# Writing out the loops of two transformer stacks and splitting 17 of every 35 wide products in two

## The chip, the cores and the metric

The kernel runs on one core of a Trainium2 chip. The metric is the device time in microseconds (us) from the kernel's start to its end. TensorE is called PE here (its weight loads PEld), VectorE DVE, ScalarE ACT, GpSimd POOL, and SP is the engine that issues the transfers.

## The reference, cut to what matters

Four layers are applied one after the other to x of shape (4, 512, 128): a retention block, a stack, a mixer with a recurrence, and the same stack again with the same weights. The change touches the stacks alone. A stack has six layers:

```python
for i in range(DEPTH):                                   # DEPTH = 6
    x = attn_layer(shift_tokens(x), Wqkv[i], ...) + x    # 16 heads of 64, window 32
    x = ffn_layer(shift_tokens(x), ...) + x              # 128 -> 341 (twice) -> 128, gated
```

The attention layer projects x to queries, keys and values (128 to 3 x 1024), normalises and rotates queries and keys, takes the softmax over a band of 64 keys, weighs the values and projects back. The feed-forward layer normalises, multiplies into two halves of 341 (a gate and a linear part), and multiplies back. Everything is float32.

## The kernel before

A stack is worked tile by tile. A tile is 128 rows of x; a sequence of 512 rows is four tiles, a layer 16, a stack 96. The kernel calls four tiles a group (`Group`, 24 in a stack). `slots` runs 96 + 16 slots, and in slot N each engine works on parts of the tiles N-3 to N-10: a software pipeline with a fixed order in each engine, written out by hand in `slot`, with one body for each place T = 0..3 of a tile in its group. PE's part of it, tile by tile:

- `project` (line 608): six products of 128 rows by 512 columns, for the parts k0, q0, k1, q1, v0, v1; `PARTS` numbers them 0 to 5.
- `turn` (line 617): four transposes for each of k0, q0, k1, q1.
- `scores` (line 632): 64 small products, 64 or 32 wide, which in float32 are 128 matrix instructions. `weigh` (line 655) is another 64, again 128 instructions.
- `project_out` (line 668): eight accumulated products of 128 columns.

Once in four tiles come `center` (line 675), `variance` (line 682), `up` (line 691, six products) and `down` (line 701, three products), each with 512 columns. So four tiles hold 24 + 1 + 1 + 6 + 3 = 35 products of 512 columns. A float32 product is two matrix instructions (the transposes are one), and each matrix instruction comes with a weight load of its own.

Behind PE, `rotate` on DVE (lines 1080 and 1082) reads each projection of a query or key from PSUM; `square` on ACT (line 881) reads the same bank when DVE has; a bank is given back to PE after that. The four work banks are handed out by the table `BANK`.

`slots` writes slots 0 to 15 out, then runs a hardware loop of two turns with a body of 32 slots, and then writes the last 32 slots out. So the loop holds 64 of the 112 slots of a stack:

```python
            run_slots(0, 0, 0, 0, 16)
            with eng.Fori(0, 2) as pair:
                run_slots(32 * pair + 16, 8 * pair + 4, 2 * pair + 1, 1, 32)
            run_slots(16 * (DEPTH - 1), 4 * (DEPTH - 1), DEPTH - 1, 1, 16 + 16)
```

In the loop the value that a wait compares with comes from a register, and `apart` puts a semaphore increment between two such waits; in code that is written out it does nothing. SP has a loop of its own over layers 1 to 4. `run` is 0 in the first stack and 1 in the second.

Of the kernel before, what the change touches and what calls it, by code (L numbers as in the profile page):

```python
# [14 lines left out]
P = 128  # L15
DIM = 128
BATCH, SEQ = 4, 512
# [3 lines left out]
DEPTH, HEADS, HD, WINDOW = 6, 16, 64, 32  # L21
# [3 lines left out]
TILES = DEPTH * BATCH * SEQ // P  # L25
# [314 lines left out]
RSQRT_SHIFT = 16  # L340
TABLE = "natural_log_exp_and_others"
GELU_TABLE = "gelu_and_others"

Group = namedtuple("Group", ("number", "layer", "row", "pair", "half"))
# [2 lines left out]
def ffn_stack(nc, shared, w):  # L348

    xo, ident, rot, mask = shared["x"], shared["ident"], shared["rot"], shared["mask"]  # L350
    with ExitStack() as ctx:
# [124 lines left out]
        def slots(eng, body):  # L476

            def run_slots(tile, group, layer, odd, slots_run):  # L480
                for n in range(slots_run):
                    def of(lag, k=n // 4):
                        return Group(group + (k - lag), layer + (k - lag) // 4, (k - lag) % 4, (k - lag) % 2,
                                     (odd + (k - lag) // 4) % 2)

                    def at(lag, n=n):
                        return tile + (n - lag), (n - lag) % 4, of(0, (n - lag) // 4)
                    body(tile + n, n % 4, group + n // 4, at, of)

            run_slots(0, 0, 0, 0, 16)  # L490
            with eng.Fori(0, 2) as pair:
                run_slots(32 * pair + 16, 8 * pair + 4, 2 * pair + 1, 1, 32)
            run_slots(16 * (DEPTH - 1), 4 * (DEPTH - 1), DEPTH - 1, 1, 16 + 16)

        block = ctx.enter_context(nc.Block())

# [1 line left out]
        def _(sp):  # L498
# [80 lines left out]
            load_mlp(0)  # L579
            sp.wait_ge(consts_set, N_CONSTS * (run + 1))  # L580
            layer_loads(0, True, False)
            with sp.Fori(1, DEPTH - 1) as layer:
                layer_loads(layer, False, False)
            layer_loads(DEPTH - 1, False, True)
            sp.wait_ge(wo_in, 16 * (layer0 + DEPTH))
# [11 lines left out]

        @block.tensor
        def _(pe):
            def project(t, T, g, c):  # L600
                if not live(t):
                    return
                if c == FIRST_IN and T == 0:
                    wait_x(pe, g.number - BATCH)
                    apart(pe, t)
                    pe.wait_ge(qkv_in, (g.layer + (layer0 + 1)) * 256)
                col = 512 * PARTS[c]
                pe.matmul(work[(BANK["p_" + c][T] + g.row) % 4][:, :], xst[:, g.row, P * T:P * (T + 1)],  # L608
                          w_qkv[:, g.half, col:col + 512], start=True, stop=True).then_inc(done["proj_" + c], 1)

            def turn(t, T, g, c):
                if not live(t):
# [58 lines left out]
            def center(g):  # L671
                if not live_group(g):
                    return
                wait(pe, "mid_set", 4 * g.number + 3)
                pe.matmul(work[(BANK["ct"] + g.row) % 4][:, :], center_m[:, :], mshift[:, g.pair, 0:SEQ], start=True, stop=True  # L675
                          ).then_inc(done["pe_center"], 1)

            def variance(g):
                if not live_group(g):
                    return  # L680
                wait_group(pe, "center_sq", g)
                pe.matmul(work[(BANK["va"] + g.row) % 4][:, :], mean_m[:, :], c_sq[:, :], start=True, stop=True  # L682
                          ).then_inc(done["pe_var"], 1)

            def up(g, kind, k):
                if not live_group(g):
                    return
                wait_group(pe, "xg_set", g)
                n = min(P, HID - P * k)
                bank = work[(BANK[("wa" if kind == "lin" else "wg") + str(k)] + g.row) % 4]  # L690
                pe.matmul(bank[0:n, :], w_1[:, g.half, 3 * (kind == "lin") + k, 0:n], x_c[:, :], start=True, stop=True  # L691
                          ).then_inc(done[f"pe_{kind}{k}"], 1)

            def down(g):
                if not live_group(g):
# [1913 lines left out]
```

## Time and profile before

| | |
|---|---|
| median of 3 runs | 3644.86 us (3643.79 to 3651.21) |
| the profiled execution: its time | 3648.2 us |
| its span, first to last instruction | 3646.4 us |
| granted TensorE clock, mean | 0.967 |
| first stack, about | 98 to 1665 us |
| second stack, about | 2083 to 3646 us |

"Span" is the time from the first to the last instruction of the profiled execution; its own time is 1.8 us longer. Where a position is given below (as at 1324.17) it is in us from the start of that span. Busy time of PE is modelled from the starts of pipelined instructions.

### The profile page before, as it was taken

To read this page: it belongs to the slowest core of one execution; us is meant where nothing else is said; L and a number is where in the kernel's file an instruction comes from. 1 tells how busy PE (TensorE), PEld (TensorE's weight loads), DVE (VectorE), ACT (ScalarE), POOL (GpSimd) and SP (SyncE) were. 2 spreads that over 40 slices of the span, in tenths; PEclk is the share of its full clock that TensorE was granted. 3 is DMA by queue.
4 is the path that set the end of the run, shared out by engine and by line. 5 is a ranking of instruction groups with operands and counts; after the bars stand their busy time and mean duration, and the time that the engine had idled before them with its cause. 6 is when DMAs were issued, how large, how long until landed. Compare 5 with 4: busy or idle time off the path is not lost. (4 is left out here: it accounts for less than half of the span.)

```text
span 3646.4 us, 153624 instructions
## 1 busy us (share of the span) xinstructions
PE 3373.7 (93%) x60144; PEld 2186.3 (60%) x60144; DVE 3341.6 (92%) x11899; ACT 2049.2 (56%) x3659; POOL 2706.3 (74%) x2440
## 2 busy tenths in 40 slices
PE   6799999999999999987699689999999999999997
PEld 4366666666666666652466446666666666666664
DVE  6899999999999999965799799999999999999995
ACT  2456666656665666644422155666666566666663
POOL 1788888888888888843144288888888888888882
PEclk9899999999999999998799699999999999999999
DMA  1233333333333333320000123333333333333332
GB/s 44 61 89 83 74 89 75 90 78 79 91 76 76 87 80 71 72 66 16 1 1 0 36 49 88 79 89 79 74 93 75 77 84 82 73 89 77 72 72 65
DMA packets 151851, 250.83 MB, mean 69 GB/s; under 512 B 42688, under 2 KB 73408, under 8 KB 150976
## 3 DMA queue, kind: packets, MB, share of 16 engines
q1 hardware_dynamic: 151104, 240.75, 27.7%
q8 instruction: 484, 7.93, 1.0%
q14 instruction: 263, 2.15, 0.2%
HBM read 38.21 MB, written 1.05 MB: 11 GB/s over the span
## 5 line engine op out<-in xcount | busy, mean ns | idle before, releaser
L608 PE MATMUL stack_work<-stack_w_qkv,stack_xst 128*128 128x512 f32 x2304 | 1173.6, 615 | 26.9 <-ACT stack_sq L881 16.7
L1337 POOL TENSOR_TENSOR stack_roped<-stack_rot_c,stack_rot_s 128x512 f32<-128x512 f32 x768 | 980.6, 1289 | 260.1 <-DVE stack_rot_s L1082 135.0
L1347 POOL TENSOR_TENSOR stack_roped<-stack_roped,stack_rnorm 128x512 f32<-128x512 f32 x768 | 791.5, 1044 | 162.4 <-DVE stack_rnorm L1114 162.4
L881 ACT ACTIVATE stack_sq<-stack_work 128x512 f32<-128x512 f32 x768 | 457.3, 595 | 735.0 <-DVE stack_rot_s L1082 727.5
L1080 DVE TENSOR_TENSOR stack_rot_c<-stack_work,rot_tables 128x512 f32<-128x512 f32 x768 | 517.0, 673 | 56.5 <-PE stack_work L608 52.0
L608 PEld LDWEIGHTS stack_work<-stack_w_qkv,stack_xst 128*128 128x128 f32 x2304 | 387.3, 193 | 300.5 <-issue 226.5
L1082 DVE TENSOR_TENSOR stack_rot_s<-stack_work,rot_tables 128x512 f32<-128x512 f32 x768 | 519.3, 676 | 1.1 <-issue 1.1
L1091 DVE TENSOR_REDUCE stack_ssq<-stack_sq 128x8 f32<-128x512 f32 x768 | 512.4, 672 | 3.3
L1125 DVE CUSTOM_DVE_ANT_0 stack_s_m<-stack_bank_s,band 128x64 f32<-128x64 f32 x3072 | 469.5, 215 | 30.1 <-PE stack_bank_s L632 26.4
L617 PEld LDWEIGHTS stack_work<-ident,stack_roped 128*128 128x128 f32 x3072 | 354.1, 141 | 167.4 <-issue 143.5
L617 PE MATMUL stack_work<-ident,stack_roped 128*128 128x128 f32 x3072 | 436.4, 277 | 19.3 <-ACT stack_sq L881 11.6
L1363 POOL TENSOR_TENSOR stack_s_m<-stack_s_m,stack_inv 128x512 f32<-128x512 f32 x384 | 412.6, 1074 | 37.8 <-DVE stack_inv L1143 37.8
L1355 POOL TENSOR_TENSOR stack_s_m<-stack_s_m,stack_smax 128x512 f32<-128x512 f32 x384 | 401.6, 1046 | 37.3 <-DVE stack_smax L1125 35.2
L655 PEld LDWEIGHTS stack_bank_o<-stack_p_pairs,stack_v_even 64*64 64x64 f32 x12288 | 330.0, 134 | 155.8 <-issue 155.6
L668 PEld LDWEIGHTS stack_work<-stack_o_t,stack_w_o 128*128 128x128 f32 x3072 | 364.5, 192 | 77.4 <-issue 63.8
L632 PEld LDWEIGHTS stack_bank_s<-stack_k_t,stack_q_t 64*32 64x32 f32 x24576 | 276.6, 105 | 206.2 <-issue 200.1
L655 PE MATMUL stack_bank_o<-stack_p_pairs,stack_v_nat 64*64 64x32 f32 x12288 | 378.2, 219 | 16.6 <-issue 16.5
L655 PE MATMUL stack_bank_o<-stack_p_pairs,stack_v_even 64*64 64x32 f32 x12288 | 378.8, 220 | 12.4 <-issue 8.8
L668 PE MATMUL stack_work<-stack_o_t,stack_w_o 128*128 128x128 f32 x3072 | 368.2, 275 | 5.2 <-issue 4.7
L632 PE MATMUL stack_bank_s<-stack_k_t,stack_q_t 64*32 64x64 f32 x24576 | 318.5, 225 | 48.0 <-issue 47.6
L655 PEld LDWEIGHTS stack_bank_o<-stack_p_pairs,stack_v_nat 64*64 64x64 f32 x12288 | 333.4, 135 | 20.2 <-issue 20.1
L907 ACT COPY stack_q_t<-stack_work 128x512 f32<-128x512 f32 x384 | 226.8, 591 | 169.0 <-PE stack_work L617 168.2
(255 smaller groups left out, 5093.2 us busy)
## 6 DMA issues: line engine op xcount, KB each, us to landing
stack_v_even<-stack_v_nat SPq DMA_DIRECT2D x768, 128.0 KB, 2.4
stack_p_pairs<-stack_p_turned SPq DMA_DIRECT2D x1536, 64.0 KB
stack_w_qkv<-table_ffn_qkv SPq DMA_DIRECT2D x192, 96.0 KB
stack_w_o<-table_ffn_wo SPq DMA_DIRECT2D x12, 512.0 KB, 3.9
stack_w<-table_ffn_w SPq DMA_DIRECT2D x12, 384.0 KB, 3.2
stack_w<-table_ffn_w SPq DMA_DIRECT2D x12, 192.0 KB, 3.0
x_outer<-L_attn_a_X SPq DMA_DIRECT2D x4, 256.0 KB, 8.1
ret_xpos<-table_xpos SPq DMA_DIRECT2D x1, 1024.0 KB, 7.5
```

Of the source, the lines that this page charges most:

```text
L608: pe.matmul(work[(BANK["p_" + c][T] + g.row) % 4][:, :], xst[:, g.row, P * T:P * (T + 1)], w_qkv[:, g.half, col:col + 512], start=True, st ...
L617: last = pe.transpose(bank[:, P * n:P * (n + 1)], roped[:, CHUNKS.index(c), T % 2, P * n:P * (n + 1)], ident[:, :])
L632: last = pe.matmul(bank_s[j][WINDOW * n:WINDOW * (n + 1), 64 * hp:64 * hp + 64], q_t[rows, T % 2, hp, WINDOW * n:WINDOW * (n + 1)], k_t[ro ...
L655: last = pe.matmul(bank_o[HD * odd:HD * (odd + 1), two, at:at + WINDOW], values[:, 2 * m + j, :], p_pairs[rows, T % 2, odd_window, j, 2 * ...
L668: last = pe.matmul(bank[:, 0:P], w_o[:, g.half, n, :], o_t[:, T % 2, n, :], start=n == 0, stop=n == PAIRS - 1)
L881: act.activation(sq[:, i % 2, :], work[(BANK["p_" + c][T] + g.row) % 4][:, :], ACT.Square).then_inc(done["squared_" + c], 1)
L1080: dve.tensor_tensor(rot_c[:, i % 2, :].rearrange("p (h d) -> p h d", h=8), src.rearrange("p (h d) -> p h d", h=8), cosine, ALU.mult)
L1082: dve.tensor_tensor(rot_s[:, i % 2, :].rearrange("p (h f d) -> p h f d", h=8, f=2), src.rearrange("p (h f d) -> p h f d", h=8, f=2)[:, :, ...
L1091: dve.tensor_reduce(ssq[:, T % 2, i, :], sq[:, i % 2, :].rearrange("p (h d) -> p h d", h=8), AX.X, ALU.add).then_inc(done["summed_" + c], 1)
L1125: last = dve.tensor_tensor_reduce(s_m[:, T % 2, j, hp, :], bank_s[j][:, 64 * hp:64 * hp + 64], mask[:, first:first + 2 * WINDOW], 1.0, LOW ...
L1337: pool.tensor_tensor(roped[:, i, T % 2, :], rot_c[:, i % 2, :], rot_s[:, i % 2, :], ALU.add).then_inc(done["roped_" + c], 1)
L1347: pool.tensor_tensor(r, r, rnorm[:, T % 2, i, :].unsqueeze(2).broadcast_to([P, 8, HD]), ALU.mult).then_inc(done["united_" + c], 1)
```

## The change

The two hardware loops become straight code: all 112 slots of a stack in every engine, and all six layers on SP. In each group 17 of the 35 products with 512 columns are issued as two products of 256 columns into the two halves of the same PSUM bank (`HALVED`; `center` and `variance` are not in it). In the first stack the first 25 projections in the order of tiles (tiles 0 to 3 and k0 of tile 4) and in the second stack the first 17 are issued as four products of 128 columns (`QUARTERED`). The semaphore is raised by the last piece, so what DVE and ACT do is as it was. And v0 and v1 get a wait for the layer's weights at the first tile of a group, which only k0 had.

```diff
+HALVED = {
+    ("gate", 1), ("gate", 2), ("k0", 1), ("k0", 2), ("k0", 3), ("k1", 0),
+    ("k1", 1), ("lin", 0), ("lin", 1), ("q0", 1), ("q0", 3), ("q1", 0),
+    ("q1", 2), ("v0", 1), ("v1", 1), ("v1", 2), ("v1", 3),
+}
+QUARTERED = (25, 17)
...
-            run_slots(0, 0, 0, 0, 16)
-            with eng.Fori(0, 2) as pair:
-                run_slots(32 * pair + 16, 8 * pair + 4, 2 * pair + 1, 1, 32)
-            run_slots(16 * (DEPTH - 1), 4 * (DEPTH - 1), DEPTH - 1, 1, 16 + 16)
+            run_slots(0, 0, 0, 0, TILES + 16)
...
-            with sp.Fori(1, DEPTH - 1) as layer:
+            for layer in range(1, DEPTH - 1):
                 layer_loads(layer, False, False)
...
+            def spans(pieces):
+                return [slice(SEQ // pieces * k, SEQ // pieces * (k + 1)) for k in range(pieces)]
...
-                col = 512 * PARTS[c]
-                pe.matmul(work[(BANK["p_" + c][T] + g.row) % 4][:, :], xst[:, g.row, P * T:P * (T + 1)],
-                          w_qkv[:, g.half, col:col + 512], start=True, stop=True).then_inc(done["proj_" + c], 1)
+                elif c[0] == "v" and T == 0:
+                    pe.wait_ge(qkv_in, (g.layer + (layer0 + 1)) * 256)
+                bank = work[(BANK["p_" + c][T] + g.row) % 4]
+                pieces = 4 if 6 * t + PARTS[c] < QUARTERED[run] else 2 if (c, T) in HALVED else 1
+                for s in spans(pieces):
+                    col = 512 * PARTS[c] + s.start
+                    last = pe.matmul(bank[:, s], xst[:, g.row, P * T:P * (T + 1)],
+                                     w_qkv[:, g.half, col:col + 512 // pieces], start=True, stop=True)
+                last.then_inc(done["proj_" + c], 1)
...
-                pe.matmul(bank[0:n, :], w_1[:, g.half, 3 * (kind == "lin") + k, 0:n], x_c[:, :], start=True, stop=True
-                          ).then_inc(done[f"pe_{kind}{k}"], 1)
+                for s in spans(2 if (kind, k) in HALVED else 1):
+                    last = pe.matmul(bank[0:n, s], w_1[:, g.half, 3 * (kind == "lin") + k, 0:n], x_c[:, s], start=True, stop=True)
+                last.then_inc(done[f"pe_{kind}{k}"], 1)
```

## Rows read from the trace of the kernel before

**Rows 1.** The page: each engine's busy us, share and instructions.

```profile
PE 3373.7 (93%) x60144; PEld 2186.3 (60%) x60144; DVE 3341.6 (92%) x11899; ACT 2049.2 (56%) x3659; POOL 2706.3 (74%) x2440
```

**Rows 2.** The page's transfer queues: kind, packets, MB, share of 16 engines.

```profile
q8 instruction: 484, 7.93, 1.0%
```

**Rows 3.** Windows, 21 groups of each stack: us, busy (count) by engine, clock, DMA.

```profile
239.89:1545.11 1305.22, 1272.38 (x25657) 838.68 (x25656) 1263.14 (x4829) 819.69 (x1470) 1108.60 (x1009) 1.00 0.34 80
2220.92:3531.07 1310.15, 1272.37 (x25657) 839.25 (x25656) 1260.78 (x4829) 819.69 (x1470) 1107.60 (x1008) 0.99 0.34 80
```

**Rows 4.** Windows of single groups, line 675's start to the next.

```profile
487.18:547.94 60.76, 60.67 (x1223) 39.72 (x1222) 60.41 (x232) 38.88 (x70) 52.80 (x49) 1.00 0.36 82
673.28:733.27 59.99, 59.99 (x1224) 39.69 (x1223) 58.59 (x230) 38.75 (x70) 51.38 (x48) 1.00 0.38 93
...
1423.26:1483.92 60.66, 60.56 (x1223) 39.78 (x1222) 60.31 (x231) 38.87 (x70) 52.96 (x49) 1.00 0.31 71
...
300.96:364.47 63.51, 60.38 (x1224) 40.07 (x1223) 61.08 (x231) 39.31 (x70) 54.41 (x50) 1.00 0.35 84
...
733.27:799.90 66.63, 62.52 (x1224) 40.59 (x1223) 60.96 (x231) 39.09 (x70) 52.77 (x49) 0.97 0.33 75
2719.70:2786.08 66.38, 62.36 (x1224) 40.43 (x1222) 59.52 (x230) 39.08 (x70) 51.20 (x48) 0.97 0.33 75
```

**Rows 5.** Waits of PE in 239.9 to 1545.1: us in total, times, longest.

```profile
PE stack_bank_s L632 <- issue: 19.0, 19, 1.7
PE stack_bank_o L655 <- issue: 8.4, 11, 1.4
```

**Rows 6.** Timeline of PE at two of its gaps: start, us, line, shape [idle before].

```profile
1324.17 0.34 PE L632 MATMUL stack_bank_s<-stack_k_t,stack_q_t 64*32 64x64 f32 x16 [0.97 <-issue]
1386.27 0.31 PE L632 MATMUL stack_bank_s<-stack_k_t,stack_q_t 64*32 64x64 f32 x7 [1.54 <-issue]
```

**Rows 7.** Windows from gap to gap.

```profile
1324.16:1386.26 62.10, 60.55 (x1257) 40.20 (x1257) 61.44 (x232) 39.00 (x70) 53.48 (x50) 1.00 0.34 80
1386.26:1495.77 109.51, 108.22 (x2135) 70.65 (x2135) 106.48 (x405) 67.49 (x121) 91.83 (x85) 0.98 0.33 75
```

**Rows 8.** Transfer queues in the window 1321.5 to 1324.3.

```profile
q8 instruction: 1, 0.02, 2.2%
```

**Rows 9.** Timeline of PE: the end of `scores` in two groups.

```profile
667.70 1.55 PE L632 MATMUL stack_bank_s<-stack_k_t,stack_q_t 64*32 64x64 f32 x120
670.38 0.32 PE L632 MATMUL stack_bank_s<-stack_k_t,stack_q_t 64*32 64x64 f32 x8 [1.14 <-issue]
...
1418.94 1.74 PE L632 MATMUL stack_bank_s<-stack_k_t,stack_q_t 64*32 64x64 f32 x128
```

**Rows 10.** Timeline at the loop's turn back in the first stack.

```profile
768.66 1.96 PE L608 MATMUL stack_work<-stack_w_qkv,stack_xst 128*128 128x512 f32 x2 [2.97 <-DMA stack_w_qkv<-table_ffn_qkv]
```

**Rows 11.** Timeline of PE: products of 512, 128 and 256 columns, one burst.

```profile
1003.98 1.02 PE L608 MATMUL stack_work<-stack_w_qkv,stack_xst 128*128 128x512 f32 x2
...
1005.71 1.88 PE L608 MATMUL stack_work<-stack_w_qkv,stack_xst 128*128 128x512 f32 x4
...
1012.83 1.51 PE L632 MATMUL stack_bank_s<-stack_k_t,stack_q_t 64*32 64x64 f32 x128
...
1031.19 3.94 PE L668 MATMUL stack_work<-stack_o_t,stack_w_o 128*128 128x128 f32 x32
1882.54 7.54 PE L2147 MATMUL scan_bank<-scan_seen,ident 128*128 128x256 f32 x16
1889.89 3.63 PE L2136 MATMUL scan_bank<-mix_kept_kkb,mix_spread 128*128 128x256 f32 x16
1893.37 1.03 PE L2136 MATMUL scan_bank<-mix_kept_r,mix_spread 128*128 128x256 f32 x4
```

**Rows 12.** Waits in 1423 to 1483, a group without a gap in PE.

```profile
ACT stack_sq L881 <- DVE stack_rot_s L1082: 14.9, 13, 2.4
...
PEld stack_work L668 <- ACT stack_sq L881: 0.9, 1, 0.9
```

More of the change, by code:

```diff
@@ L674, in center @@
                 wait(pe, "mid_set", 4 * g.number + 3)
-                pe.matmul(work[(BANK["ct"] + g.row) % 4][:, :], center_m[:, :], mshift[:, g.pair, 0:SEQ], start=True, stop=True
-                          ).then_inc(done["pe_center"], 1)
+                bank = work[(BANK["ct"] + g.row) % 4]
+                for s in spans(2 if ("center", 0) in HALVED else 1):
+                    last = pe.matmul(bank[:, s], center_m[:, :], mshift[:, g.pair, s], start=True, stop=True)
+                last.then_inc(done["pe_center"], 1)
             def variance(g):
@@ L681, in variance @@
                 wait_group(pe, "center_sq", g)
-                pe.matmul(work[(BANK["va"] + g.row) % 4][:, :], mean_m[:, :], c_sq[:, :], start=True, stop=True
-                          ).then_inc(done["pe_var"], 1)
+                bank = work[(BANK["va"] + g.row) % 4]
+                for s in spans(2 if ("variance", 0) in HALVED else 1):
+                    last = pe.matmul(bank[:, s], mean_m[:, :], c_sq[:, s], start=True, stop=True)
+                last.then_inc(done["pe_var"], 1)
             def up(g, kind, k):
```

## The prediction

> **What bounds the kernel now.** I read the page first. PE is busy 93% and DVE 92% of the span [rows 1]; an average says no more than that both are near their limit somewhere, so I cut the trace into periods. Line 675 (`center`) runs once in four tiles, and from one of its starts to the next is one group of a stack. Each stack has 21 such periods in its steady part, 1305.2 and 1310.2 us long [rows 3]: 62.15 and 62.39 us a group, 62.27 in the mean. The 42 periods make 2615.4 us, 72% of the span. The rest is the filling and draining of the two pipelines, the retention and the mixer, where PE waits for other engines most of the time.
>
> The single periods show what the mean hides [rows 4]. PE's work is the same in each, 1222 matrix instructions. The shortest takes 59.99 us with PE busy throughout. Six periods have hardly a gap in PE; they last 59.99 to 60.76 us, 60.5 in the mean. Most others last 61 to 64 us, the one at 300.96 for instance 63.51, and PE is still busy only 60.38 of that. Two, with the loop's turn back in them, last 66.63 and 66.38.
>
> Where the gaps lie is in PE's waits [rows 5]: 19 gaps with 19.0 us in front of `scores` instructions, 11 with 8.4 us in front of `weigh` instructions, in the first stack alone, all put down to "issue". Nothing that the profile records releases them, so neither data nor a semaphore is late. The reader is to see where they sit [rows 6]: inside a burst, between two equal instructions, with nothing to wait for; these two are 0.97 and 1.54 us long.
>
> The distances tell the cause [rows 7]. From the gap at 1324.17 to that at 1386.27 PE runs 1256 matrix instructions and 1256 weight loads (the view counts one more that overlaps the edge), 2512 rows of its program. 
>
> I walked this count of rows through the whole trace. In straight code, and inside the loop, every "issue" gap of over 0.25 us in a steady period lies within two rows of one residue modulo 256. A boundary early in a burst costs nothing, one in the last third of a burst or just behind it 0.3 to 1.7 us. A group has 2490 rows when written out and 2502 to 2513 in the loop, so its ten or nine boundaries drift by 50 to 70 rows from group to group, and each group pays another sum.
>
> **What the change does to this.** *Splits.* Each product that is split adds two matrix instructions and two loads, 4 rows: 17 x 4 = 68. The wait added to v0 and v1 at the first tile falls beside a wait that is there, so each makes one row: 2. With the 2490 of the written-out group that is 2560, ten blocks exactly. So the boundaries stand still: what the first steady group pays, all 42 pay.
>
> *Where they stand.* The start of the program is untouched, so I carry the residue over from the first stack of before (194, counted from the first row in the trace) and count the new order in, quarters and all. In numbers of the old 1222 matrix instructions of a group, from line 675, the ten boundaries fall at 104, 228, 346, 473, 596, 714, 836, 956, 1078 and 1203, in the second stack 2 to 3 later. Before, the group at 673.28 had its nine at 104, 229, 352, 475, 603, 727, 852, 976 and 1099, and it is the one of 59.99 us without a gap [rows 4]. Eight of the ten new places lie within 20 of its own, in the first half of a burst or in products. Two need a look. At 596, in `project_out`, the block lasts some 7.6 us, and of its neighbours the four at 591 did not stall, and of the four at 603 and 608 two did, by no more than 1.4 us, the longest in `weigh` [rows 5]. At 1203, 6 instructions ahead of the end of `scores`, the block before begins at 1078 and lasts only some 3.5 us (two products of 0.86 and most of a burst of 1.74); a boundary at 1202 cost 1.14 us where the block had begun at 1075 (the gap after 120 of 128 instructions), and no gap where it had begun at 1076 (the burst at 1418.94 is whole) [rows 9]. I take 0 for both, with 1.1 as the other end.
>
> *Price of the splits on PE.* Two more matrix instructions of 512 columns add 1.88 - 1.02 = 0.86 us, 0.43 each. With 256 columns 12 more add 3.63 - 1.03 = 2.60 us, 0.217 each [rows 11]. A split product is 4 x 0.217 = 0.87 us, so 0.01 more: 0.2 us a group and 8 us in 48 groups if PE sets the pace. The other end is line 2147, also 256 columns, at 7.54 / 16 = 0.47 us: 17 x 4 x 0.25 = 17 us a group. Its moving operand is another array, read in another pattern; line 2136 has the form of the split product (128 rows, 256 adjacent columns of an SBUF table, a load each), so I take its price. The quarters cost 8 x 3.94 / 32 - 0.86 = 0.12 us each at most, 42 of them 5 us, in the filling of the pipeline, where PE has gaps: 0 to 5, I take 1.
>
> *The loops.* The turn back stands in two periods, the first with a gap of 2.97 us in PE at 768.66 [rows 10]; the view names a transfer of weights as releaser, but in the three other layer changes of the stack that transfer is never late, so I read it as the branch. The granted clock is 0.97 of full in both [rows 4], so after the gap PE runs for a while at 1.2 GHz instead of 2.4, and its busy time is 62.5 us in place of 60.4: 2 us more. Both periods become like the others. The waits in the loop's registers cost nothing I can see: periods without a gap last 59.99 and 60.76 in the loop and 60.66 written out [rows 4].
>
> The Trainium skill ("Runtime: NRT & Kernel Launch", section "Instruction fetch mechanics") says that a program streams in blocks of 16 KiB, 256 instructions, and that crossing into the next costs a queue bump that is mostly hidden, because instructions are issued more slowly than blocks come in. The block's size agrees with the trace, 16.4 KB a packet; that crossings are hidden does not, with up to 1.7 us at some [rows 2, 5]. By the page alone the alignment would bring nothing (the second rival's sum).
>
> *What is late next.* With PE's gaps gone DVE is in the way. In the group at 1423.26 it is busy 60.31 of 60.66 us, at 487.18 60.41 of 60.76 [rows 4]. There ACT waits 14.9 us for DVE's rotations, and PE's weight loads wait for ACT's squares, one for 0.9 us [rows 12]. So a group can't go to PE's 59.99 for long; in that one DVE is busy only 58.59 us, having caught up in the gaps of the group before. The six periods without gaps hold this already, and since DVE sets the pace in them the 0.2 us of splits don't add to it in full. I take 60.6 us.
>
> **Sum.** 42 x 60.6 = 2545.2 against 2615.4: 70 us less. Filling and draining: 1 us for the quarters, and some of the four larger gaps in the draining may go or come, 0. From the profiled execution's 3648.2 that is 3578; the runs' median is 3.3 below it, 3644.9 - 70 = 3575.
>
> **Rivals.** (1) *The gain is there but smaller: 61.0 to 61.9 us a group.* Either the boundary at 1203 (or the one behind 596) costs 1.1 us in every group, or DVE takes longer: it is busy 61.08 us in the group at 300.96 [rows 4]. For it speaks that a fixed boundary has no good groups to average with. Against it speaks the neighbour at 1076. 42 x 61.4 = 2579, 36 us less: 3609; from 3588 to 3630.
>
> (2) *Boundaries are not the cause; nothing changes.* Then only the turns back go (66.63 and 66.38 down to 62.1: 9 us) and the splits cost 8: about 3644. Against it stand distances of 2560 and 4352 rows.
>
> (3) *Slower: the boundaries fall badly, in all groups.* If my count of rows is off by half a burst (some 80 rows, say because rows that the trace doesn't show change ahead of the stacks), each group is like the worst, 63.5 us [rows 4], with PE short by 3.1 us: 42 x (63.5 - 62.27) = 52 us more, 3697. It decides from a mean of 62.3, that is 1.8 us of stalls a group. For it: one place sets all 42 groups. Against it: of the 40 groups without a turn back only ten last over 63 us.
>
> (4) *Better: DVE keeps up and groups take 60.0.* 95 us less, 3550.
>
> **Chances.** The forecast (3556 to 3588) 0.62, rival 1 0.22, rival 2 0.04, rival 3 0.06, rival 4 0.06. Two runs' medians tell 0.2%, 7 us, apart. The range runs from 3552 into the middle of rival 1, 3615; the likeliest case's own is 3556 to 3588. Faster by over 0.2% 0.91, within it 0.03, slower 0.06.
>
> **What the profile after would show.** Periods of line 675 nearly equal, near 60.6 us, none of 66. Instruction packets 490 to 500. "issue" gaps inside `scores` and `weigh` gone from the steady part, or all at the same instruction of each group, which would be rival 1 or 3. Pairs of 256 columns at 0.217 us. DVE busy over 99% of a group, and PE's loads waiting for ACT's squares in most groups. The prediction is wrong if the stalls come at places where none stood before (what makes a block late is then not its place alone), or if a split product costs more than 0.9 us.

## The result, and the profile after

The changed kernel takes **3597.4 us** in the median of 4 runs (3585.8 to 3608.3), beside 3644.3 for the kernel before in 4 runs on the same chip: a ratio of 0.9867, with a 95% interval from 0.9827 to 0.9907. The forecast was 3575 with a range from 3552 to 3615. The profiled execution is the slowest of the four, 3608.3 us, with a span of 3606.2 us, so it may show more stalls than a typical run.

The page, its engines and the queue of instructions; they answer to [rows 1, 2]:

```profile
PE 3381.6 (94%) x61984; PEld 2523.7 (70%) x61984; DVE 3344.1 (93%) x11899; ACT 2043.2 (57%) x3659; POOL 2704.4 (75%) x2440
...
q8 instruction: 493, 8.08, 1.0%
```

The same 21 steady groups of each stack as in [rows 3], from the first start of `center` (now line 689) to the last:

```profile
239.00:1519.70 1280.70, 1270.51 (x26372) 971.75 (x26371) 1262.63 (x4829) 816.67 (x1470) 1106.63 (x1008) 1.00 0.35 81
2201.80:3490.10 1288.30, 1274.40 (x26371) 974.75 (x26370) 1263.66 (x4830) 816.61 (x1470) 1107.62 (x1009) 0.99 0.34 81
```

2569.0 us in place of 2615.4, 46.4 us less: 61.17 us a group, where 60.6 was forecast and 62.27 stood before. The two profiled executions are only 40.2 us apart in span, since the rest of the kernel took 6.2 us more in this one; in the repeat below it took 6.2 us less than before (1024.8 against 1031.0), so that part is scatter as far as these runs tell. PE's busy time is as before, 2544.9 us, though some 8 us more were forecast for the splits; the period less PE's busy time, which is PE's idle time, went from 70.6 to 24.1 us. DVE's work is unchanged, as it should be.

Three single groups, as in [rows 4]. The first is among the shortest (60.18 us is the least), the second is the median; no period of 66 us is left, and the last row is one of five over 62.8:

```profile
665.40:725.60 60.20, 60.20 (x1257) 46.26 (x1256) 59.27 (x231) 38.96 (x70) 52.23 (x49) 1.00 0.38 95
604.40:665.40 61.00, 60.47 (x1257) 46.02 (x1256) 60.65 (x232) 38.83 (x70) 52.93 (x49) 1.00 0.32 74
...
2634.10:2697.00 62.90, 60.82 (x1257) 46.28 (x1256) 61.06 (x231) 38.72 (x70) 53.02 (x49) 1.00 0.37 91
```

What is left of PE's waits for "issue" in the bursts, first stack, then second (us, times, longest), against [rows 5]:

```profile
PE stack_bank_s L644 <- issue: 5.6, 16, 0.6
PE stack_bank_o L667 <- issue: 3.3, 3, 1.6
...
PE stack_bank_o L667 <- issue: 7.9, 7, 1.5
PE stack_bank_s L644 <- issue: 4.6, 12, 0.7
```

Small waits in `scores` (line 644), many of them, and few large ones in `weigh` (line 667). But for one gap in the first group of each stack (1.56 us at 243.11, 1.34 at 2205.80, in `weigh` too), they stand at two places of the group and nowhere else: the boundary that the prediction puts at 1203, and the one at 714, which ends the block that begins at 596. These are the two that the prediction says "need a look" (it names the second by the block's begin, 596, and its 7.6 us) and takes at 0. The boundaries do stand still: in the first stack the gaps come after 730 and 1234 of a group's 1256 matrix instructions, in the second after 727 to 733 and 1231 to 1237, and each of them is at row 193 modulo 256 of the program or one beside it.

The price of a split, on PE's timeline: 8 and then 4 products of 256 columns, as in [rows 11]:

```profile
2486.97 1.89 PE L619 MATMUL stack_work<-stack_w_qkv,stack_xst 128*128 128x256 f32 x8
...
2668.46 1.03 PE L708 MATMUL stack_work<-stack_x_c,stack_w 128*128 128x256 f32 x4
```

4 more take 0.86 us, 0.215 each: 0.86 for two products, as unsplit.

### The profile page after: what moved, and what is told of

Read it like the earlier page. It is cut to its first block and busy times, and to the rows that moved or that the text cites. A ratio compares the mean times of both kernels' runs of the same rounds, so it can differ in the third digit from the quotient of the medians.

```text
span 3606.2 us, 155076 instructions
## 1 busy us (share of the span) xinstructions
PE 3381.6 (94%) x61984; PEld 2523.7 (70%) x61984; DVE 3344.1 (93%) x11899; ACT 2043.2 (57%) x3659; POOL 2704.4 (75%) x2440
## 5 line engine op out<-in xcount | busy, mean ns | idle before, releaser
L619 PE MATMUL stack_work<-stack_w_qkv,stack_xst 128*128 128x256 f32 (+2 forms) x3760 | 1182.3, 444 | 20.9 <-ACT stack_sq L898 15.7
L619 PEld LDWEIGHTS stack_work<-stack_w_qkv,stack_xst 128*128 128x128 f32 x3760 | 656.0, 197 | 147.4 <-issue 39.8
L708 PE MATMUL stack_work<-stack_x_c,stack_w 128*128 128x256 f32 (+2 forms) x960 | 307.9, 439 | 13.7 <-ACT stack_x_c L988 7.3
```

Source lines behind the costliest of these rows:

```text
L619: last = pe.matmul(bank[:, s], xst[:, g.row, P * T:P * (T + 1)], w_qkv[:, g.half, col:col + 512 // pieces], start=True, stop=True)
```

## Why a block is late

A stall in `weigh`, on PE's timeline (start, us, line, shape, idle before in brackets):

```profile
2670.72 0.29 PE L667 MATMUL stack_bank_o<-stack_p_pairs,stack_v_nat 64*64 64x32 f32 x7
2672.50 0.19 PE L667 MATMUL stack_bank_o<-stack_p_pairs,stack_v_nat 64*64 64x32 f32 x1 [1.48 <-issue]
```

The block that PE works off there began at 2663.22. SP in the same stretch issues transfers back to back:

```profile
2660.21 0.51 SPq L546 DMA_DIRECT2D stack_p_pairs<-stack_p_turned  x1
...
2664.56 0.59 SPq L547 DMA_DIRECT2D stack_p_pairs<-stack_p_turned  x1
2665.19 1.08 SPq L504 DMA_DIRECT2D stack_w_qkv<-table_ffn_qkv  x2
2666.38 2.41 SPq L528 DMA_DIRECT2D stack_v_even<-stack_v_nat  x4
2672.50 0.51 SPq L546 DMA_DIRECT2D stack_p_pairs<-stack_p_turned  x1
```

14 issues about 0.63 us apart, until 2668.79. The instruction packet starts at 2669.65, 6.43 us after the block's boundary and 0.9 us after the last of these issues. In the group before it, in which PE does the same instructions and doesn't stall, the boundary is at 2602.69 and the packet starts 2.59 us later, at 2605.28, in the middle of SP's train:

```profile
2602.89 0.59 SPq L546 DMA_DIRECT2D stack_p_pairs<-stack_p_turned  x1
2603.52 0.59 SPq L547 DMA_DIRECT2D stack_p_pairs<-stack_p_turned  x1
2604.22 3.69 SPq L528 DMA_DIRECT2D stack_v_even<-stack_v_nat  x4
```

Those four issues take 3.69 us in place of 2.41: the third alone, at 2605.42, lasts 1.85. So this packet started between two of SP's issues, and the other behind all of them.

From the packet's end until PE goes on, 1.4 us pass (1.37 to 1.44 in the mean of each kernel of this study, over 370 stalls in all). That gives a rule for one boundary: stall = start of the packet after the block's first row + its duration + 1.4 - PE's work in the block.

| stall at | packet starts | lasts | PE's work | rule | measured |
|---|---|---|---|---|---|
| 946.29 | 6.15 | 1.66 | 7.87 | 1.34 | 1.49 |
| 2239.90 | 6.45 | 0.92 | 7.54 | 1.23 | 1.22 |
| 2364.06 | 6.04 | 1.18 | 7.80 | 0.82 | 0.95 |
| 2672.50 | 6.43 | 1.45 | 7.80 | 1.48 | 1.48 |

Over the 417 boundaries of the steady groups of after, the rule and the measured stalls correlate at 0.98 and sum to 17.9 and 16.9 us; in the other kernels with the loops out the correlation is 0.96 to 0.995, where there are more than two stalls. So the rule says how large a stall is once the packet's start is known; what sets that start is another question. At the boundary in question the packet starts between -0.6 and 6.5 us; 7 of 42 came late enough. A block has two ways to be late: short work (3.5 us before the boundary at 1203) with a prompt packet, or long work with a packet that came behind SP's train. I count, among 420 boundaries of after, 229 at which SP was just issuing such a train: 83 of their packets started over 1.5 us later. Of the 191 others 4 did. Before, 56 of 62 us of stalls stand behind packets that started over 1.5 us late.

Two limits of this count. A train is not enough: 76 of the 83 late packets belong to two of the ten places, the block begun at 596 (35 of 42) and the one begun at 1203 (41 of 42); at the eight others a train ran at 145 boundaries and 7 packets were late. And it is not needed: with the boundaries elsewhere, packets also start over 1.5 us late where no train runs, 33 of 254 in the bad phase below, 34 of 211 with the loops out and nothing split, 48 of 205 with the engines' loops out. What delays those, no run here shows.

## The experiments

Steady groups are those of [rows 3]; "idle" is their length less PE's busy time, "1.2 GHz" the time in them in which the trace records TensorE's granted clock at half.

| kernel | median us | ratio to before (95%) | us a group | idle | 1.2 GHz |
|---|---|---|---|---|---|
| before | 3644.3 | 1 | 62.27 | 70.6 | 23.9 |
| after | 3597.4 | 0.987 (0.983 to 0.991) | 61.17 | 24.1 | 20.5 |
| after, again | 3600.1 | 0.988 (0.986 to 0.990) | 61.39 | 27.0 | 27.4 |
| loops out, no split | 3603.7 | 0.990 (0.988 to 0.992) | 61.29 | 38.5 | 3.4 |
| bad phase | 3620.6 | 0.993 (0.991 to 0.995) | 61.59 | 60.3 | 3.4 |
| other phase | 3588.1 | 0.985 (0.982 to 0.987) | 60.83 | 15.5 | 0 |
| SP's loop out | 3653.7 | 1.000 (0.999 to 1.001) | 62.43 | 76.0 | 20.4 |
| engines' loops out | 3612.5 | 0.989 (0.987 to 0.991) | 61.40 | 46.7 | 3.4 |
| short trains | 3586.4 | 0.982 (0.980 to 0.984) | 60.98 | 31.3 | 0 |
| (14, 13) | 3586.0 | 0.981 (0.979 to 0.984) | 60.79 | 13.7 | 0 |
| TensorE's loop out | 3624.4 | 0.995 (0.993 to 0.997) | 61.81 | 57.3 | 10.2 |
| the other three's | 3641.6 | 0.999 (0.997 to 1.001) | 62.00 | 69.2 | 6.8 |
| (14, 13), DVE lighter | 3538.3 | 0.971 (0.969 to 0.974) | 59.93 | 2.8 | 0 |
| (14, 13), 4 loads | 3587.2 | 0.986 (0.983 to 0.988) | 60.95 | 18.8 | 3.4 |

Three chips were used, one for each block of four; before took 3644.1, 3653.3 and 3645.4 us beside them, so kernels of different blocks are compared by their ratios.

### First block: are the boundaries the cause?

**The changed kernel, unchanged**, for its scatter.

> The changed kernel once more, unchanged, beside the three below on one chip. Its four runs so far lie at 3586, 3589, 3606 and 3608 us. Theory A (blocks of 256 rows; in most groups the block that begins at matrix instruction 714 is there in time, in a few it comes late by chance): again 3585 to 3610, and in the profile the 'issue' gaps of over 1 us in the steady part all stand at that one place, but in other groups than before. Theory B (the writing-out of the loops is what helped): nothing to say against a steady 3597.

3600.1 us. Executions of this kernel lie between 3586 and 3608 in both sets of runs. In the two profiled executions five and six periods are over 62.8 us, and in nearly all of those there is a stall in `weigh` with a clock that falls behind it.

**The loops written out and nothing split.**

```diff
-            run_slots(0, 0, 0, 0, 16)
-            with eng.Fori(0, 2) as pair:
-                run_slots(32 * pair + 16, 8 * pair + 4, 2 * pair + 1, 1, 32)
-            run_slots(16 * (DEPTH - 1), 4 * (DEPTH - 1), DEPTH - 1, 1, 16 + 16)
+            run_slots(0, 0, 0, 0, TILES + 16)
...
-            with sp.Fori(1, DEPTH - 1) as layer:
+            for layer in range(1, DEPTH - 1):
```

> The kernel before with its loops written out, and nothing split. A group has 2490 rows, so the block boundaries move on by 70 rows from group to group. Theory A: the groups pay what their boundaries happen to fall on, 1.3 us in the mean by the places where the kernel before stalled, so 61.7 us a group and 3615 to 3635 us; periods between 60.5 and 63.5 us. Theory B (register waits and branches cost, or the looped code does): all of the gain is here, 3590 to 3600. If only the turns back were the loops' price, 3635.

3603.7 us, better than I expected and within 4 us of the changed kernel on the same chip. Most of the gain is not that of the splits. The splits do what they are for: idle time is 38.5 us here and 24 to 27 with them. But most of it is given back, since in the changed kernel the granted clock falls to 1.2 GHz behind its stalls in `weigh` (27.4 us of that in the profile of the same block, against 3.4). This kernel has stalls in `weigh` too, 7.5 us in 11 gaps over 0.25 us, but only two of them are as long as about 1.2 us, and the clock falls behind one.

**Two other phases**: each product more that is quartered in the filling of the pipeline adds 12 rows where it was whole and 8 where it was halved, and all boundaries behind it come that much earlier in the code: 40 rows for the bad phase, 112 rows later in the first stack and 104 in the second for the other.

```diff
-QUARTERED = (25, 17)
+QUARTERED = (29, 17)   # bad phase
+QUARTERED = (14, 18)   # other phase
```

> The changed kernel with 29 quartered projections in the first stack instead of 25, in the filling of the pipeline; the steady code is the same instruction for instruction, but its block boundaries come some 44 rows earlier in it, at matrix instructions 84, 208, 326, 453, 580, 694, 817, 936, 1062 and 1183 of the old count. Theory A: boundaries at 580 (end of one scores burst) and 1183 (in another) stall by 1.3 and 1.5 us in every group of both stacks, periods of 63 to 64 us, 3670 to 3710 us in all. Theory B, or any in which the split products or the missing loops gave the gain: 3597, as the changed kernel.

> The changed kernel with 14 and 18 quartered projections instead of 25 and 17: boundaries at 32, 157, 282, 402, 528, 643, 765, 891, 1012 and 1131. Theory A: the gaps at 714 and at 1203 are gone; by the places where the kernel before stalled only 402 should cost, 0.3 us a group, so 60.6 to 60.9 us a group and 3575 to 3595 us. Theory B: 3597.

The bad phase takes 3620.6 us, 20.5 more than the changed kernel. So the place matters, and the sign is as expected, but the size is under a third of it (70 to 110 us more were expected). Of the two places expected to stall, 580 and 1183, only the first does. It has 42 gaps over 0.8 us, one in every group, and 39 of them are of one kind, a short block (2.0 us of work) with a prompt packet; the timeline, and then the waits of the two stacks:

```profile
507.94 1.47 PE L644 MATMUL stack_bank_s<-stack_k_t,stack_q_t 64*32 64x64 f32 x125
510.82 0.30 PE L644 MATMUL stack_bank_s<-stack_k_t,stack_q_t 64*32 64x64 f32 x3 [1.41 <-issue]
...
PE stack_bank_s L644 <- issue: 28.1, 23, 1.8
...
PE stack_work L708 <- issue: 29.7, 21, 1.8
```

A stall of 1.4 us in every group makes groups of 61.59 us, only 1.0 over the 60.6 that the forecast takes for DVE's limit; and the clock hardly ever falls behind these gaps. The groups of 63.5 us on which I had priced this case have two or three stalls each (the one at 300.96: 0.41, 1.03 and 1.68 us).

The other phase takes 3588.1 us, the lower half of what was expected. Its two stacks, and all waits for "issue" of the first:

```profile
238.30:1512.60 1274.30, 1270.03 (x26372) 965.51 (x26371) 1266.67 (x4829) 815.49 (x1470) 1107.11 (x1009) 1.00 0.35 82
2190.60:3471.00 1280.40, 1269.14 (x26372) 965.69 (x26371) 1269.12 (x4830) 815.92 (x1470) 1107.45 (x1009) 1.00 0.34 82
...
PE stack_work L619 <- issue: 0.9, 3, 0.5
PE stack_work L680 <- issue: 0.4, 1, 0.4
PE stack_bank_s L644 <- issue: 0.4, 1, 0.4
```

The first stack is at 60.68 us a group with 1.7 us of stalls in all: the forecast's 60.6, reached by boundaries that stand elsewhere.

The second stack says more than the total. Its boundaries stand at the first one's places to within one matrix instruction (one block, for instance, begins after 785 of a group's 1256 in the first and 784 in the second, and ends after 912 and 911), and yet it has 7.3 us of stalls over 0.25 us where the first has 1.3, most of them behind this block:

```profile
PE stack_work L619 <- issue: 6.8, 15, 0.9
```

At this place one of 21 groups of the first stack stalls by more than 0.25 us, and 11 of 21 of the second. Packets start 0.63 us before the block's first row in the mean in the first and 0.44 in the second, and the blocks have 2.01 and 1.91 us of work: with margins this small the rule gives a stall in one stack and none in the other. The place alone does not.

### Second block: which loops, and what makes packets late

**SP's loop alone written out, then those of the four compute engines alone.** Each is one of the two hunks above.

> The kernel before with only SP's loop over layers written out; the loops of the other engines stay. In the kernel before, 56 of 62 us of the stalls over 0.25 us that stand on a block boundary follow an instruction packet that started more than 1.5 us after the boundary, and SP's loop body issues transfers 0.659 us apart in its trains, against 0.640 us where it is written out. Theory S (it is SP's loop that makes the packets late, so writing it out gives the gain of e1_loops_out): 3600 to 3615 us. Theory T (the gain came from the loops of the engines, by the turn-backs and the places of the boundaries): 3638 to 3648 us, as before. I lean to T.

> The kernel before with the loops of the compute engines written out and SP's loop kept. Theory T: 3600 to 3612 us, two turn-backs gone (2.97 and 2.61 us of stall and a stretch at 1.2 GHz behind each) and the rest from other places of the boundaries. Theory S: 3638 to 3648 us. Both shares added (e4 and e5 each give part of 40 us) would read as 3615 to 3630 in each.

Clean: 1.000 and 0.989. SP's loop costs nothing, the loops of the four compute engines cost all of the 40 us. The two stacks of the second kernel, where [rows 3] have 1305.22 and 1310.15 with PE busy 1272.4:

```profile
241.20:1528.70 1287.50, 1264.34 (x25658) 835.25 (x25657) 1266.59 (x4829) 817.74 (x1470) 1108.14 (x1009) 1.00 0.34 81
2204.00:3495.50 1291.50, 1267.96 (x25657) 836.80 (x25656) 1268.62 (x4830) 817.35 (x1470) 1108.25 (x1009) 1.00 0.34 81
```

**Short trains.** The 8 transfers that fill `p_pairs` for a tile become 4 of twice the size.

```diff
-                for window in range(4):
-                    rows = slice(WINDOW * window, WINDOW * (window + 1))
...
+                for window in range(2):
+                    rows = slice(2 * WINDOW * window, 2 * WINDOW * (window + 1))
+                    sp.dma_start(p_pairs[rows, b, window, :, :, :], p_turned[rows, 1, :, :, :]).then_inc(p_in[b], 16)
+                    sp.dma_start(p_pairs[rows, b, 1 - window, :, :, :], p_turned[rows, 0, :, :, :]).then_inc(p_in[b], 16)
```

> The kernel after with the 8 transfers of 32 partitions that fill p_pairs for a tile issued as 4 of 64 partitions, so that SP's trains are of 8 or so transfers instead of 12 to 14; the same bytes move, but two windows of each pair change places, so the probabilities that weigh reads aren't the right ones. Theory L (the stall in weigh, boundary 714, comes from an instruction packet that waits for the end of SP's train): the late packets (78 of 167 in weigh) become few, the stalls in weigh go (8 to 12 us of stall and 10 to 14 us of 1.2 GHz clock behind them), 3583 to 3592 us, with less scatter. Rival P (the packet is late for another reason, or the place alone decides): 3595 to 3602 us, as the kernel after, with 7 to 11 stalls in weigh.

3586.4 us, 0.982 against 0.987 and 0.988: theory L's time. At the block begun at 596, packets over 1.5 us late fall from 35 of 42 (31 in the repeat) to 21, and no 1.2 GHz is left in the steady groups. But only about half of the stall time in `weigh` goes (5.1 us in the two stacks, against 8.0 and 12.5), and `scores` has more. Both stacks:

```profile
PE stack_bank_s L642 <- issue: 11.7, 19, 1.0
PE stack_bank_o L665 <- issue: 2.0, 3, 0.9
...
PE stack_bank_s L642 <- issue: 11.6, 21, 1.0
PE stack_bank_o L665 <- issue: 3.2, 4, 1.2
```

So the link from SP's issues to the packet's start is borne out at that block: the median start goes from 3.1 us (3.5 in the repeat) to 1.6. It isn't for the whole: packets over 1.5 us late are 94 of 420 here, 87 in after and 99 in the repeat, since those of other blocks become more. And the gain doesn't come from gone stalls: PE's idle time in the steady groups is 31.3 us, more than the 24.1 and 27.0 with long trains, and what fell is PE's busy time (2529.8 us against 2544.9 and 2551.6), with no 1.2 GHz left. What else the larger transfers changed wasn't measured by itself.

**Another place for the second stack's boundaries**, with QUARTERED = (14, 13). The expectation below takes this for the first stack's phase; it is not. That one the second stack already had in the other phase. Here five products fewer are quartered, which moves its boundaries 52 rows later in the code: they stand after 56, 182, 308, 435, 561, 682, 806, 936, 1063 and 1186 matrix instructions of a group, where the first stack has them after 32, 157, 284, 409, 534, 658, 785, 912, 1038 and 1162.

> The kernel after with QUARTERED (14, 13) instead of (25, 17): the second stack's boundaries stand at the same places of a group as the first stack's in e3_other_phase, which had 1.7 us of stall in 21 groups where the second had 7.1. Theory A (place of the boundaries decides in both stacks alike): second stack 1274 to 1277 us for 21 groups, 3580 to 3584 us in all. Rival: the second stack differs by something else (its transfers, its start), and stays at 1280 us: 3586 to 3590 us.

3586.0 us and 0.981. Its second stack takes 1277.9 us, between theory A's 1274 to 1277 and the rival's 1280, and the first 1275.2. It tests neither, as the places aren't the first stack's: its stalls are 6 in `weigh` with 4.1 us, of which the first stack has none. It has the lowest ratio of all kernels that do the whole computation; with the other phase's 0.985 on another chip the intervals overlap, so the last step isn't shown by the total; the second stack is 2.5 us shorter in one profiled execution of each.

### Third block: the loop's share, and the next limit

**TensorE's tile loop alone written out, then those of ACT, DVE and POOL alone.**

> The kernel before with the tile loop of TensorE's program alone written out; the loops of ACT, DVE, POOL and SP stay. Theory P (the gain of e5 is in TensorE's own instruction stream: a group in the loop has 11 register instructions and 2502 to 2508 rows against 2490, and a stall of 2.4 to 3.2 us a group where the written-out one has 0.9 to 1.6 at the same phase): the ratio of e5, 0.987 to 0.991, so 3605 to 3620 us beside a before of 3653, 3600 to 3610 beside one of 3644. Rival V (it is the loops of the other engines, DVE's above all, whose register instructions and turn-backs delay TensorE): ratio 0.998 to 1.001.

> The kernel before with the tile loops of ACT, DVE and POOL written out and those of TensorE and SP kept: the other half of e8. Theory P: ratio 0.997 to 1.001, no gain. Rival V: 0.987 to 0.991. If the two halves each give part of it: 0.993 to 0.997 in both.

0.995 and 0.999: 20 us (12 to 27) and 4 us (-2 to 9), where all four together give 41 (33 to 49). Neither theory has it right. TensorE's own loop costs half, the others nothing as long as TensorE's stays, and the rest only goes when both are out. The trace of the first of the two shows a part of why. DVE and PE at the place where the others turn back (their branches stand at 766.6 to 767.5):

```profile
770.60 0.69 DVE L1083 TENSOR_TENSOR stack_rot_c<-stack_work,rot_tables 128x512 f32<-128x512 f32 x1 [3.23 <-issue]
774.23 1.97 PE L620 MATMUL stack_work<-ident,stack_roped 128*128 128x128 f32 x8 [2.33 <-ACT stack_sq L884]
```

With PE's loop gone, PE waits 2.3 us here for a square that waits for DVE, and 6.8 us at 1.2 GHz begin beside that gap. With PE's loop in, PE's own turn-back makes a gap of 2.97 us at the same place [rows 10], so that taking the others' away gains nothing. In all, PE waits 6.9 us for ACT's squares in these steady groups and 1.0 us with all engines' loops out.

**DVE lighter.**

```diff
-                dve.tensor_reduce(ssq[:, T % 2, i, :], sq[:, i % 2, :].rearrange("p (h d) -> p h d", h=8),
+                dve.tensor_reduce(ssq[:, T % 2, i, :], sq[:, i % 2, 0:256].rearrange("p (h d) -> p h d", h=8),
```

> e7_best_phase with each sum of squares on DVE (16 a group, 0.67 us each) taken over 256 of its 512 columns, so that the norms are those of half the data; DVE has about 5.4 us a group less to do. Theory B (DVE and TensorE are nearly level, TensorE's own work is 60.0 to 60.3 us a group where DVE's is 60.7): 12 to 28 us less than e7, ratio 0.974 to 0.978. Rival D (DVE alone holds the group at 60.7 and TensorE has room): over 100 us less, ratio under 0.955. Rival N (DVE isn't the limit): within 5 us of e7, ratio 0.980 to 0.983.

3538.3 us, 0.971: a little beyond theory B and far from both rivals. Its two stacks:

```profile
234.50:1492.70 1258.20, 1256.52 (x26372) 966.20 (x26371) 1220.97 (x4829) 819.68 (x1470) 1106.79 (x1009) 1.00 0.35 83
2158.90:3417.60 1258.70, 1257.62 (x26372) 969.19 (x26371) 1202.76 (x4829) 821.08 (x1470) 1106.05 (x1009) 1.00 0.35 83
```

PE is busy 2514.1 of 2516.9 us: 59.93 us a group is PE's pace with hardly a gap, and a lighter DVE lets it go 0.86 us faster than the 60.79 of (14, 13). The reduction takes 0.406 us in place of 0.672, so 4.3 us a group less for DVE; PE could use only 0.86 of it. Two things fell with it. PE's modelled busy time is 25.3 us less with the same instructions (2539.4 before), so it holds time that PE waited, and can't be taken for pure work. And packets over 1.5 us late are 34 of some 420 in place of 77, with PE's idle time at 2.8 us in place of 13.7, though SP issues as many transfers as before: so up to 0.26 of the 0.86 us may be stalls and not DVE. Of the 52 us between the spans 36 are in the steady groups, the rest in filling, draining and between the stacks.

**Few loads.** (14, 13) with the next layer's w_qkv in 4 transfers in place of 16.

```diff
-                        if n < 8:
-                            load_qkv(layer + 1, 2 * n)
-                            load_qkv(layer + 1, 2 * n + 1)
+                        if n < 8 and n % 2 == 0:
+                            load_qkv(layer + 1, n // 2)
```

> e7_best_phase with the next layer's w_qkv loaded in 4 transfers of 384 KB instead of 16 of 96 KB, so that the longest of SP's trains have 13 transfers instead of 14 or 15, and in half of the tiles 12. Theory L (packets are late by the length of the train that they meet): few of the stalls of e7 are left there, so 0 to 5 us less than e7, ratio 0.979 to 0.982. Rival H (large transfers hold the DMA engines, so that the instruction packet or the small transfers beside it take longer): over 3 us more than e7, with more late packets.

3587.2 us, 0.986, with 9 stalls in `weigh` of 7.5 us where (14, 13) has 6 of 4.1. No gain, and packets over 1.5 us late are 73, hardly fewer than 77. By the ratio rival H would be right, by the microseconds there is no difference; the two ran on different chips, and I can't separate them.

## Why the prediction came out as it did

**The cause of the gaps: right.** Packets of 256 rows. The rows a group came out as counted, 2560: the gaps stand at the same instructions of each group, and there are 493 packets, within the 490 to 500. Moving the boundaries by 40 rows (bad phase) costs 20 us, by some 110 the other way gains 12. One gap of the trace of before doesn't fit "every 'issue' gap lies within two rows of one residue": the first of 64, 0.78 us at 247.63, is at row 167 modulo 256 where the next ones are at 193 and 194, and what it is stays open.

**The places: right, their stalls not.** Both boundaries with a question mark stall. The step that failed is "I take 0 for both", a term of the sum that was too small. At 1203 it is 0.25 to 0.7 us in every other group, 8.9 us in sum; how much of that DVE would have taken anyway isn't shown. At 714 it is 1.0 to 1.5 us in 6 groups and 0.5 in one, and behind 4 of these the granted clock falls for a recorded 3.4 us each. The prediction held the place of a boundary to be enough. It isn't: at 714 the packet starts between -0.6 and 6.5 us after the block's first row, and that hangs at least in part on SP's transfers, a queue that the prediction didn't look at. Neighbouring gaps in the trace of before were read as "two did, by no more than 1.4 us"; that it depended on something else than the place was there to be seen. The prediction's own sign of being wrong, stalls at places where none stood before, didn't come; what it was to stand for (a block is not late by its place alone) is true all the same. Of the 0.57 us a group between 60.6 and 61.17, stalls of 16.9 us make up to 0.40, and 20.5 us at half clock cost up to 10 us, 0.24. So the range held the result, but the forecast, 22 us too low, did not.

The Trainium skill ("Runtime: NRT & Kernel Launch", section "Instruction fetch mechanics") calls the crossing mostly hidden. 388 of the 417 crossings of after agree with that; the other 29 are those at which the packet's start, its 1.2 us and 1.4 more exceed the work of one block.

**The loops: wrong.** "The waits in the loop's registers cost nothing I can see" rests on groups without a gap; and the loop was given 9 us, for its two turn-backs, in the second rival's sum. Written out alone they give 40 us. The turn-backs are part of it. The same page of the Trainium skill warns in that section that a taken branch breaks the sequential prefetch; the gap of 2.97 us [rows 10] agrees, and with such a gap gone in each stack it is at most some 9 us. The rest is fewer stalls in the groups and less time at 1.2 GHz behind them (23.9 us before, of which 6.8 stand behind the turn-backs, and 3.4 with all engines' loops out): 64 boundary stalls with 61.9 us before, 69 with 67.0 with SP's loop alone out, 47 with 44.3 without TensorE's loop, 46 with 40.5 with all engines' loops out. Packets start perhaps somewhat later where TensorE loops, 1.5 to 1.6 us after the boundary in the mean of before and 1.3 to 1.45 in those without. But a looped group also has other rows (some 2503 against 2490), so the boundaries fall at other places, and whether the places or the loop's own rows make the difference no run here separates. The two kernels without TensorE's loop have the same PE program and nearly the same stalls; of the 17.4 us between their steady groups 5.9 are PE's waits for squares, seen in the third block, and the rest is spread over stalls and busy time. So the measured time fell into the range partly by luck: of 44 us on one chip, 40 come with the loops alone, to which the sum of 70 us gives some 9, and the alignment, which was to bring most of it, brings 4 more, 16 at the other phase's places.

**DVE as the next limit: right in the main.** DVE is busy 60.65 of 61.00 us in a typical group, 98.3% over all 42 where over 99% was expected, and taking 4.3 us of its work away moves groups to 59.93. Its nearness would also explain why a stall of 1.4 us costs 1.0, and why alignment was worth less than the sum of its stalls; that is argued, not shown. Rival 4's 60.0 is PE's pace with the lighter DVE to 0.1 us.

**The splits: right.** 0.215 us a piece against 0.217; the other end, 17 us a group, didn't come.

**The rivals.** What came lies inside rival 1's range, 3588 to 3630, near its lower edge: groups of 61.17 where it says 61.0 to 61.9, in part for the reason it names: the boundary at 1203 costs something, though 0.2 us a group and not 1.1. Rival 3's mechanism exists, its price was 52 us more than before and proved to be 24 less: 0.993 of before with a stall in each group. Rival 2, no effect of boundaries, is refuted by the phases, though its remark that the loops count by themselves was nearer than its 9 us.

**What it would take to do better.** A better phase alone: 0.981 to 0.985. Below 60.7 us a group only the lighter DVE brought it here, to 59.9.

## What to carry to other kernels

Where an engine stalls with "issue" and no releaser, count rows to the gaps modulo 256, then compare for each block the start of its instruction packet plus duration plus 1.4 us with the engine's work in that block; short bursts of tiny matmuls are where it shows. Look at what delays the packet too: beside trains of back-to-back transfer issues on another queue one and the same boundary stalled in one group and not in the next. Before aligning, write the loops out and measure that alone: here it gave 40 of 44 us, and a change that bundles both hides which one paid.

## What the runs showed of the hardware

- PE goes on 1.4 us after its instruction packet ends (means of 1.37 to 1.44 in 12 profiles), the packet takes 1.2 us in the mean, and it starts a median 0.9 us after the block before it begins: a block that PE works off in under about 3.5 us stalls at such a start. In the other phase packets started 0.4 to 0.6 us before the block in front, and blocks of 2.0 us then stalled in 1 of 21 groups, those of 1.9 us in 11 of 21.
- In the changed kernel instruction packets start late beside SP's transfer issues: 83 of 229 started over 1.5 us late while SP issued a train, 4 of 191 otherwise, and beside one that started in a train an issue of 0.6 us lasted 1.85. 76 of the 83 stand at two of ten places, and in other kernels packets were late without a train as well (48 of 205), so this is one cause and not the rule.
- In the two profiles of the changed kernel the granted clock fell to 1.2 GHz after 13 of the 14 gaps of 1.2 us and more that stand in `weigh` in the steady groups (the one at 2672.50, shown above, is the exception); in the twelve other profiles it fell after 6 of 19 such gaps in `weigh` and after 7 of 122 elsewhere. In the bad phase, after 42 gaps of 1.36 us in the mean at the end of `scores` and in `up`, it fell once. So the place of a gap doesn't settle it either. Total idle time doesn't say what the clock does: 24 us of idle came with 20.5 us at half clock, 60 us of idle with 3.4.
- With PE's loop written out a group has some 11 register instructions and 2 to 4 waits fewer on PE, and the kernel takes 20 us less; which of these, or the moved boundaries, makes the time isn't shown.
